# Two waits of GpSimd inside a gather group are taken out (graph attention, mixer and experts on one core)

## The reference

```
xn = layernorm(x)
x  = x + gnn(xn, edges) + mix(xn)          # attention over edges; per node mixer
x  = x + ffn(layernorm(x))                 # 8 experts, each three 256x256 products, weighted by softmax

gnn: h = xn @ W + b, 8 heads of 32
     e = leaky_relu(h_src[src] + h_trg[trg]);  p = exp(e - max(e))
     out[n] = sum over edges into n of h[src] * p / sum of p       # self loops included
mix: u = batchnorm(conv(log map(xn)));  relu; depthwise and grouped 1x1 products
     out = (v k^T) q / sum(v), per group of 32;  then a 512x256 product and a norm
```

## Time and profile before

| | before |
|---|---|
| runs | 1182.02, 1184.98, 1188.89 us |
| the profiled execution | 1176.66 us, of this span 1174.9 us |
| gather stage, first to last gather | 67.5 to 668.8 us |
| groups 6 to 28, from one L1202 to the next, mean | 17.8 us |
| TensorE's mean granted clock | 0.923 |
| busy: TensorE, VectorE, ScalarE, GpSimd | 83%, 67%, 45%, 32% of the span |

### The profile page before, as it was taken

How to read it: one execution, slowest core, us unless ns; L and a number is a source line. 1 busy time by engine, 2 the same in 40 slices (tenths; PEclk the granted TensorE clock), 3 DMA queues, 4 the chain that set the end, 5 groups by cost and what they waited for, 6 DMA issues and landing times.

```text
span 1174.9 us, 15618 instructions
## 1 busy us (share of the span) xinstructions
PE 973.4 (83%) x5483; PEld 838.3 (71%) x5483; DVE 787.9 (67%) x1394; ACT 529.1 (45%) x1088; POOL 380.3 (32%) x408
## 2 busy tenths in 40 slices
PE   0998477878878888888764558999999999999996
PEld 0776356766767767766653447889978899998986
DVE  6786557777877977879787874676555454554544
ACT  1200034444444444444432135656655666667663
POOL 0034755666666666666676500000000000000000
PEclk9997779999998898999977777999999999999999
DMA  7332433434334343443447410000000000000012
GB/s 208 115 88 73 135 97 112 115 105 118 109 112 122 102 121 98 117 118 106 116 117 214 140 51 5 1 1 1 16 13 1 28 21 8 27 1 1 1 37 74
DMA packets 51375, 89.39 MB, mean 76 GB/s; under 512 B 10454, under 2 KB 34346, under 8 KB 51277
## 3 DMA queue, kind: packets, MB, share of 16 engines
q0 software_dynamic: 18768, 52.88, 16.6%
q1 hardware_dynamic: 32509, 35.27, 9.5%
HBM read 81.42 MB, written 6.68 MB: 75 GB/s over the span
## 4 chain that ended last, share of the span: by engine, by line
PE 55%; DVE 20%; issue 12%; ACT 6%; another core or an unknown queue 4%; DVEq 1%; DMA 1%; SPq 0%; ACTq 0%; POOL 0%; POOLq 0%
PE bank L872 12%; PE bank L873 11%; PE bank L874 11%; PE bank L750 5%; DVE U L1310 4%; DVE G L1202 3%; PE bank L788 3%; PE bank L680 2%; PE bank L709 2%; PE bank L799 2%; ACT junk L490 2%; PE bank L813 2%; DVE oh L1190 1%; PE bank L939 1%
## 5 line engine op out<-in xcount | busy, mean ns | idle before, releaser
L428 POOL DMA_INDIRECT G<-projected_rows,src_l x391 | 376.9, 964 | 288.9 <-issue 106.6
L750 PE MATMUL bank<-G,oh 128*128 128x264 f32 x782 | 201.9, 409 | 73.4 <-issue 38.9
L1473 DVE TENSOR_TENSOR hil<-hid,hil 128x1024 fp32r<-128x1024 f32 (+2 forms) x112 | 121.9, 1089 | 201.8 <-ACT hil L621 201.7
L750 PEld LDWEIGHTS bank<-G,oh 128*128 128x128 f32 x782 | 153.3, 201 | 111.4 <-issue 51.3
L613 ACT ACTIVATE hid<-bank,faff 128x512 f32<-128x512 f32 (+2 forms) x224 | 158.9, 722 | 151.6 <-PE bank L874 149.6
L872 PE MATMUL bank<-ew,hil 128*128 128x256 f32 (+1 forms) x400 | 113.5, 284 | 1.5 <-DVE feat_rows L1485 1.5
L873 PE MATMUL bank<-ew,hil 128*128 128x256 f32 (+1 forms) x400 | 113.0, 283 | 0.0
L874 PE MATMUL bank<-ew,hil 128*128 128x256 f32 (+1 forms) x400 | 113.0, 282 | 0.0
L621 ACT CAST hil<-hid 128x1024 fp32r<-128x1024 f32 (+2 forms) x112 | 105.3, 940 | 9.8 <-ACT hid L613 0.4
L1202 DVE TENSOR_TENSOR G<-G,bank 128x3072 f32<-128x3072 f32 (+1 forms) x33 | 109.0, 3304 | 0.0
L788 PEld LDWEIGHTS bank<-feat_rows,wqkv 128*128 128x128 f32 x600 | 82.6, 210 | 20.1 <-ACT TT L504 12.0
(11 more groups left out here) (289 smaller groups left out, 1656.4 us busy)
## 6 DMA issues: line engine op xcount, KB each, us to landing
dstb<-targets SPq DMA_DIRECT2D x32, 384.0 KB
G<-projected_rows,src_l POOLq DMA_INDIRECT x391
projected_rows<-sums SPq DMA_DIRECT2D x25, 132.0 KB, 3.6
x_in<-in_x SPq DMA_DIRECT2D x3, 1024.0 KB, 8.3
U<-in_x SPq DMA_DIRECT2D x24, 128.0 KB
out<-feat_rows SPq DMA_DIRECT2D x24, 128.0 KB
TT<-in_W SPq DMA_DIRECT2D x8, 256.0 KB
wqkv<-in_W SPq DMA_DIRECT2D x8, 256.0 KB
```

The source lines that it names most:

```text
L428: g.indirect_dma_start(out=G[slot][:, c, :], out_offset=None, in_=table[:, :], in_offset=bass.IndirectOffsetOnAxis(ap=src_l[:, grp, c:c + ...
L750: ins = T.matmul(b_seg[g % 2][:, 0:ROW], oh[g % 2][:, c, :], G[g % SLOTS][:, c, :], start=(c == 0), stop=(c == ch - 1))
L1473: V.tensor_tensor(hidl[layer][par][:, :, 0:cols], hid[layer][:, :, 0:cols], hidh[layer][par][:, :, 0:cols].bitcast(F32), ALU.subtract).the ...
```

## The change

GpSimd's two waits inside a group are taken out. The twelve gathers of a group are then issued one after the other, and GpSimd waits in front of a group only. No other engine's stream is changed.

```
             def gather(grp):
-                slot, t = grp % SLOTS, grp - LEAD - MIX0
+                slot = grp % SLOTS
                 need(pool, s["g_free"], grp - SLOTS + 1)
                 ...
                 need(pool, s["seg_ready"], grp - LEAD)
                 for c in range(CHUNKS[grp]):
-                    if c == 5:
-                        need(pool, s["hte_ready"], grp - LEAD + 2)
-                    if c == 9 and 0 <= t < NT:
-                        pool.wait_ge(s["u_mm"], 3 * t + 3)
                     g.indirect_dma_start(
```

## The result

The changed kernel is slower: 1238.49 us, the median of four runs (1229.38 to 1246.37), against 1183.5 for the kernel before. The ratio is 1.046, 95% interval 1.042 to 1.051. The forecast was 1228, from a sum of 44 us on top of the kernel before; the medians lie 55 us apart.

What follows compares the result with a forecast made beforehand. No engine is full, so a loop of waits sets the pace. Only the wait at c == 9 was priced, 10 x 4.4 = 44 us, giving 1220.7 on the profiled run, 1229 on the median; forecast 1228 us, range 1182 to 1252.

Steps and rivals of the forecast that it cites:

- The mechanism: TensorE's instruction stream and increments are held while gathers are in flight, and let go when the last outstanding gather lands.
- Rival 2: At GpSimd's wait before the tenth gather: TensorE's release doesn't depend on the gathers, so nothing changes, 1185 us; chance 0.12.
- rival 3: Group behind a gated one: GpSimd's pace sets the loop, each gives back 1.98 us, 20 us faster, 1165; chance 0.07.
- Rival 1: In the hold, the third increment leaks from TensorE's crawl; only TensorE's remainder comes later: 27 us, 1212; chance 0.17.
- The 11 ends: Group ends where ScalarE waited for TensorE and went on 2.10 to 2.51 us after the last gather, mean 2.35.
- (a): GpSimd inside a group: both waits go, gathers follow every 1.25 us, met waits cost nothing visible; price 0.
- (b): Wait at c == 9, late in 10 groups: without it the release comes 4.4 us later, adding 44 us.
- (c): Wait at c == 5, late once, in group 21: removal costs 0 to 8.8 us; taken as 0, 9 for the range.
- (d): Waits in front of a group stay, so GpSimd can't run on without end: price 4.4 and not 15 us.
- (e): TensorE's clock after longer holds: `u_rows` 1.4 us slower in each of 10 groups; taken as 0, 14 for the range.
- rival 4: A later TensorE takes the hold mid-sums in every group: 4.4 us in up to 24 groups, 105 us, 1290; chance 0.09.

Runs made afterwards that it cites:

- pause_c9_again: Changed kernel plus six chained GpSimd memsets before the tenth gather of groups 4 to 28, on chip C: 1180.3 us, ratio 0.994 to the kernel before.
- gate_at_11: Kernel before with the wait for `u_mm` moved from the tenth to the twelfth gather, chip A: 1210.18 us, ratio 1.029.
- c9_only: Kernel before with only the wait at c == 5 taken out, the one at c == 9 kept, chip A: 1186.31 us, ratio 1.007.
- c5_only: Kernel before with only the wait at c == 9 taken out, the one at c == 5 kept, chip A: 1218.12 us, ratio 1.032.
- gate_at_7: Kernel before with the wait for `u_mm` moved from the tenth to the eighth gather, chip A: 1184.15 us, ratio 1.006.
- no_branch_again: Changed kernel with TensorE's two branches over empty loops in each group also left out, chip C: 1265.18 us, ratio 1.064 to the kernel before.
- after_again: The changed kernel, unchanged, run once more on chip D: 1118.3 us, ratio 1.001 to the kernel before.

## Why the prediction was right, and where its terms were off

**The mechanism** holds in what the forecast used: a hold of TensorE lasts until GpSimd pauses or has issued its last gather. `pause_c9_again` shows it with no wait in it, and `gate_at_11` shows the dose. "Held while gathers are in flight" says too much: during the first six or more gathers of a group TensorE all but never stands, and the hold begins behind a load by SyncE (last section). Rival 2 (1185, no dependence) and rival 3 (faster) are out by the result. The rule on turns between queues that the prediction took from the Trainium skill (DMA: Bandwidth & Descriptors, Queues, rings and completion order) would have given rival 2 if the hold were a refill waiting behind the gathers; whether it is one no run shows, so the result speaks against that time and not against the rule. Rival 1 (1212), that the third increment leaks out of the crawl, fails too: `mix` itself came 4.2 us later. But increments do leak now and then. The 11 ends that the prediction counted leave out that of group 19 of before, where ScalarE went on 0.86 us behind the last gather and not 2.1 to 2.5.

**(a)** The twelve gathers stand 1.25 us apart without a gap, and the first nine of 24 groups are 2.2 us shorter in all. Right.

**(b)** 4.4 us were forecast for each held group. Measured are 6.67 - 2.49 = 4.18 us up to `mix` and 4.06 up to the next group. The count was 12 and not 10. That makes 49 us where I had 44. The waits of 8 to 9 us in front of L1300 came (7.9 to 9.7 but for one of 6.4), its lag behind the last gather was 1.9 to 4.0 us rather than 2.1 to 2.5: ScalarE often has two squares left to do after the release, as in group 11. A part of (b) was right by luck. I took the next group to follow 5.1 us after the release as before. Counted from `mix` it does (4.37 and 4.48 us), but for another reason: before, the sums' records end at 384.06, 2.7 us ahead of the next gather; in after, the sums at half clock fill that time.

**(c)** Taken as 0 with 9 us for the range. `c9_only` says 0.7%, 7 to 8 us: the size was near the end of the range. The reason I gave, that this gate was late only once, missed that it works as a reserve: it bites when TensorE's turn and the gathers stand otherwise to each other, twice each in `c5_only` and `gate_at_11` and in 9 groups of `gate_at_7`. That it was late only once in before because the other gate kept TensorE up is argued and not shown.

**(d)** No group ran on without end, but this is the step that failed in size. "Nothing that follows is nearer than before, the whole loop shifts" was true for the gated group and false for the one behind it: 1.7 us in each of 12, 20 us in all, since TensorE's lateness carries the next hold out of `mixed_out` into the sums. That is rival 4's mechanism, of which I had expected 4.4 us in a few groups; it came as a smaller price in all of them, and in its full shape only in `no_branch_again`.

**(e)** Taken as 0 with 14 for the range, priced by `u_rows` only. `u_rows` did not get slower (391 ns a matmul, 412 before). The clock fell where TensorE came out of the longer hold, in the sums: 472 ns against 390 over 576 matmuls, and that is on the path, as GpSimd waits for them. How much of the 20.5 us in the groups between is clock no run separates, but the trace gives an estimate. Where matmuls of the sums follow each other at once, they start 227 ns apart at the full clock and 463 at the low one. In the 12 groups between, 41 of them ran at the low clock in after, which is 41 x 0.236 = some 10 us, about half. In the held groups it was 112; before had one such pair in all.

## What to carry to other kernels

A wait that guards no data can still earn its time, by what stops while it waits; before it is taken out, look at what the others do during its pause, and whether their releases lie at its end. Where an engine crawls beside many small gathers, a pause of about 2 us in their issue (1.8 was tried) is worth a try, but a tuning of this kind holds for the chips that show the crawl. And price a shift once more for the group behind: ask which wait the same hold will meet when it falls a few us later.

## What the runs showed of the hardware

**Chips differ.** The same kernel before took 1179.65 and 1186.64 us on A and C, 1116.15 and 1117.85 on B and D, 6% less, and the changed kernel 1118.3 on D against 1238.49 where the case was measured, 10% less. Program, DMA traffic and spacing of the gathers are the same. The difference lies where the gathers are: of the 125.8 us between the profiled runs of after and `after_again`, 110.3 lie between the starts of groups 5 and 29. On B and D none of the six kernels that were traced showed a hold, and no edit of gates or branches moved the time by more than 0.3% (the pauses cost 0.6%). Each chip was measured in one session, so whether it is the chip or something else that went with it, such as where the tables lie in memory, isn't shown.

**What holds TensorE** stays open. It is not the taken branches of TensorE alone (`no_branch_again`), and not the gathers' bandwidth alone (241 GB/s beside a full TensorE on D). Two things in the trace of after narrow it. Here are its queues (packets, MB, share of 16 engines) in group 11, from 298.9 to 301.2 us, from 301.7 to 307.6, which is the hold, and from 309.9 to 311.1:

```profile
q1 hardware_dynamic: 143, 0.39, 51.1%
q0 software_dynamic: 67, 0.22, 31.9%
...
q0 software_dynamic: 240, 0.68, 42.2%
...
q8 instruction: 1, 0.02, 5.0%
```

First, the queue q1 carries SyncE's load of `dstb` (384 KB). In all 23 groups from 5 to 27 TensorE's hold begins 0.7 to 5.3 us after the first packet of that load; before it, with six to eleven gathers already issued, TensorE's stands over 0.3 us come to 3.2 us in all 23 groups together. The long crawl of groups 2 and 3 of before fits too: it began at 124.2 us, behind a load from 120.4 to 122.4, and outlived the load by 26 us. So gathers alone didn't start a hold there; what the load has to do with it is untested, as no run moves or splits it. In `after_again` the same load lies beside the same gathers and nothing is held. Second, that it is the fetching of instructions is only argued, and the packets give it little support: in 18 of the 23 holds the instruction queue q8 moved nothing, and in the groups 5 to 14 its next packet came 1.0 to 2.6 us after TensorE had run on.

**The clock after a hold.** In group 11 of after TensorE got 0.50 (1.2 GHz) from 308 to 310 us, behind a hold (301.7 to 307.6) in which it had been busy 1.86 us of 5.9, and the sums' rest cost 468 ns a matmul. TensorE's mean granted clock fell from 0.923 to 0.889 in the profiled runs, and was 0.940 in `after_again`.
